# A vision tower: all four score pairs of a half ahead of the feed-forward tiles

## The reference, cut to what matters

```python
for l in range(LAYERS):                       # LAYERS = 6
    keys = jnp.concatenate([past, x], axis=1)
    q = (x @ Wq.T + bq).reshape(B, T, HEADS, HEAD_DIM)        # 16 heads of 16
    k = (keys @ Wk.T + bk).reshape(B, T + H, HEADS, HEAD_DIM)
    v = (keys @ Wv.T + bv).reshape(B, T + H, HEADS, HEAD_DIM)
    scores = jnp.einsum('bqhd,bkhd->bhqk', q, k) / jnp.sqrt(jnp.asarray(HEAD_DIM, x.dtype))
    scores = jnp.where(valid[None, None], scores, neg)
    attn = jax.nn.softmax(scores, axis=-1)
    o = jnp.einsum('bhqk,bkhd->bqhd', attn, v).reshape(B, T, C)
    o = o @ Wo[l].T + bo[l]
    x = _ln(x + o, ln1_g[l], ln1_b[l])
    ff = jax.nn.gelu(x @ W1[l].T + b1[l], approximate=False) @ W2[l].T + b2[l]   # 256 -> 1024 -> 256
    x = _ln(x + ff, ln2_g[l], ln2_b[l])
```

## Time and profile before

| what | us |
|---|---|
| median of 3 runs | 821.38 (821.06 to 822.22) |
| span of the profiled execution | 819.1 |
| TensorE busy in it | 801.5 |
| VectorE busy | 633.9 |
| ScalarE busy | 460.6 |
| GpSimd busy | 251.6 |

### The profile page before, as it was taken

One profiled execution on the slowest core, in us unless ns is written; L12 is line 12 of the kernel. 1 busy time (PEld: TensorE's weight loads), 2 busy tenths in 40 slices (PEclk: granted clock), 3 DMA queues, 4 the chain that ended last, 5 costly groups with the idle time before them and its releaser, 6 DMA issues.

```text
span 819.1 us, 16629 instructions
## 1 busy us (share of the span) xinstructions
PE 801.5 (98%) x6060; PEld 751.4 (92%) x6060; DVE 633.9 (77%) x1287; ACT 460.6 (56%) x829; POOL 251.6 (31%) x297
## 2 busy tenths in 40 slices
PE   9999999999999999999999999999999999999988
PEld 8998789999999999899999989999998999999758
DVE  5786693778778876778797887878778787876796
ACT  4386424433333336585786777667687767745421
POOL 0002120410111100364366147335525623633020
PEclk9999999999999999999999999999999999999999
DMA  5010946998889812010210021031012103010001
GB/s 191 1 52 1 373 124 253 328 323 310 317 309 337 321 53 107 1 40 14 100 44 0 17 98 38 13 102 38 4 39 72 38 13 102 26 82 1 1 0 30
DMA packets 18290, 88.36 MB, mean 108 GB/s; under 512 B 3120, under 2 KB 7472, under 8 KB 12240
## 3 DMA queue, kind: packets, MB, share of 16 engines
q1 hardware_dynamic: 18256, 87.90, 30.4%
HBM read 85.05 MB, written 2.84 MB: 107 GB/s over the span
## 4 chain that ended last, share of the span: by engine, by line
PE 47%; issue 23%; POOL 18%; DVE 8%; ACT 3%; DMA 1%; POOLq 0%; SPq 0%; DVEq 0%; ACTq 0%
PE bank L1139 14%; POOL W_L L2000 7%; PE bank L1176 6%; POOL HF_L L2058 4%; POOL arena L1981 3%; POOL WQKV_L L2000 3%; PE bank L746 2%; PE bank L872 2%; PE bank L1185 2%; PE bank L722 2%; PE bank L1049 2%; PE bank L788 1%; POOL SQ L2019 1%; PE bank L1123 1%; PE bank L1490 1%
## 5 line engine op out<-in xcount | busy, mean ns | idle before, releaser
L1139 PE MATMUL bank<-arena 128*128 (+1 forms) x1024 | 117.8, 274 | 0.0
L1139 PEld LDWEIGHTS bank<-arena 128*128 128x128 f32 x1024 | 117.4, 192 | 0.0
L1981 POOL TENSOR_TENSOR arena<-arena,srec 111x456 f32<-111x456 f32 x56 | 52.3, 962 | 125.1 <-DVE srec L2153 125.1
L2000 POOL TENSOR_TENSOR W_L<-LW,W_H 128x256 fp32r<-128x256 f32 x96 | 68.5, 752 | 36.9 <-DVE XHL L2589 33.5
L2058 POOL TENSOR_TENSOR HF_L<-arena,HF_H 128x296 fp32r<-128x296 f32 x48 | 43.8, 937 | 76.7 <-ACT HF_H L1896 76.7
L788 PE MATMUL bank<-XHL,W_H 128*128 128x296 f32 x288 | 65.1, 307 | 0.0
L1896 ACT ACTIVATE arena<-bank,vec 128x296 f32<-128x296 f32 x96 | 48.8, 509 | 20.4 <-PE bank L788 15.4
L2012 POOL TENSOR_TENSOR QW<-QW,arena x14 | 22.4, 1600 | 119.0 <-DVE QW L2490 65.6
L1330 PE MATMUL bank<-HF_L,W_H 128*128 128x296 f32 x192 | 57.4, 299 | 0.0
L1330 PE MATMUL bank<-HF_H,W_H 128*128 128x296 f32 x192 | 57.4, 299 | 0.0
L1330 PE MATMUL bank<-HF_H,W_L 128*128 128x296 f32 x192 | 57.3, 299 | 0.0
(11 more groups left out here) (276 smaller groups left out, 2205.4 us busy)
## 6 DMA issues: line engine op xcount, KB each, us to landing
arena<-ew_in SPq DMA_DIRECT2D x16, 2048.0 KB, 9.0
arena<-ew_in SPq DMA_DIRECT2D x16, 1024.0 KB, 7.0
LW<-lw_in SPq DMA_DIRECT2D x12, 1024.0 KB, 5.0
arena<-route SPq DMA_DIRECT2D x32, 185.0 KB, 3.2
LW<-lw_in SPq DMA_DIRECT2D x6, 768.0 KB, 4.3
fp_weights<-arena SPq DMA_DIRECT2D x1, 2048.0 KB, 6.4
arena<-fp_weights SPq DMA_DIRECT2D x1, 2048.0 KB, 7.2
arena<-patches_in SPq DMA_DIRECT2D x2, 864.0 KB, 7.4
```

The lines of the kernel that those rows point to most:

```text
L1139: last = mm(o[:, m * CAP:(m + 1) * CAP], w[:, kc, mi * P:(mi + 1) * P], xg(kc, e), start=(kc == 0), stop=(kc == C - 1))
L1981: nc.gpsimd.tensor_tensor(v, v, srec[0:QROWS, s:s + 2, :].unsqueeze(3).to_broadcast([QROWS, 2, C * JH, KEYS]), ALU.mult).then_inc(p_ready, 1)
L2000: last = nc.gpsimd.tensor_tensor(low[:, cols], value[:, cols], high[:, cols], ALU.subtract)
```

## The change

All four pairs of scores stand ahead of the first `f1` tile, both in the list that deals out the banks and in the row that TensorE issues. Before, pairs 0 and 1 stood there, pair 2 behind tiles 0 and 1, and pair 3 behind tiles 2 and 3.

```diff
@@ phase_order
     att("v", 0, 1, 2, 3)
-    att("s", 0, 1)
+    att("s", 0, 1, 2, 3)
     for i in range(4):
         ffn("f1", 2 * i, 2 * i + 1)
-        if i < 2:
-            att("s", 2 + i)
     ffn("f2", 0, 1)
@@ phase, TensorE
                 if x:
-                    for i in range(2):
+                    for i in range(HB // 2):
                         scores(rx, plan, p0 + i)
                 if y:
                     pe.wait_ge(wl_ready["w1"], ly + 1)
...
                     if not x and i == 1:
                         turn_x(0)
-                    if x and i < 2:
-                        scores(rx, plan, p0 + 2 + i)
                 if y:
                     pe.wait_ge(wl_ready["w2"], ly + 1)
                     down()
```

## The result

| | before | after |
|---|---|---|
| median of the runs of one comparison, us | 821.36 (5 runs, 821.06 to 822.22) | 828.11 (5 runs, 827.95 to 828.73) |
| ratio, 95% interval | | 1.0084 (1.0072 to 1.0096) |
| span of the profiled execution, us | 819.1 | 826.9 |
| first score of the first double step to the last product of the last feed-forward, us | 403.08 | 410.07 |
| first score to down projection, half 0 in the feed-forward, us | 10.78 | 11.39 |

The change costs 6.75 us between the medians; 828.2 us was forecast. The spans differ by more, 7.8 us: the first double step's first score starts at 352.90 us before and at 353.74 after, 0.84 us that arise ahead of all that the change touches. In the traces of the eleven experiments, with either order of the scores, this start lies between 353.19 and 353.78 us, so the trace of before was an early one. From there on it is 6.99 us.

What follows compares the result with a forecast made beforehand. TensorE, busy 98% of the span, was taken as the bound, with VectorE's shifts (1.08 us a pair against 0.82 us a tile) making it wait: 6 x 0.60 + 5 x 0.64 = 6.8 us on 821.4 gives 828.2 us, range 823.5 to 830.2 us.

Steps and rivals of the forecast that it cites:

- three waits for shifts: TensorE's tiles 3, 4 and 5 wait for VectorE's shifts 1, 2 and 3: nearly 0, 0.17 and 0.38 us.
- the first wait: Tile 3 could start at 500.70, when shift 1 ends, and starts at 500.76: nearly 0.
- 6 x 0.60 + 5 x 0.64: Down projection starts 0.60 us later in six steps and 0.64 us later in five: 6.8 us in all.
- The restarts: TensorE's starts after waiting for a shift, taken as pair 3's restart shows: 0.06 us behind the shift's end.
- the two bounds: Waiting tile loses nothing at its start, 0.9 us less; or three waits each cost another 0.06 us, 2.0 us more.
- The 2.3 us that the prediction puts around the span: Median of 821.4 us less the profiled span of 819.1 us, said to be untouched by the change.
- the wait of 0.34 us: TensorE's wait for GpSimd's normalise before the last transpose (513.32): said to stay and hide nothing, products and chain moving alike.
- ScalarE's pace: Rival: sixteen gelus start 1.98 us later and end 0.08 or 0.33 us later; 2.1 us, 823.5 us; chance 0.08.
- TensorE's row alone: Rival: evacuations always over in time, step costs 10.50 us on TensorE; 1.8 us less, 819.6 us; chance 0.05.
- Its condition: For the rival on TensorE's row: shift 3 ends before tile 5's own turn, 502.34, and gelus take under 0.39 us.
- Low halves beside GpSimd's pieces of the weights: Rival: meeting on SBUF doubles VectorE's two low halves, 0.75 us in six steps; 4.5 us, 832.7 us; chance 0.03.
- The clock: Rival: short waits halve TensorE's clock for the tiles, 5.2 us a step, 57 us, 885 us in all; chance 0.02.

Runs made afterwards that it cites:

- experiment 1: Kernel after, with VectorE's shift 3 put ahead of the low halves of tiles 0 and 1: 825.40 us, ratio 1.0048.
- experiment 2: Kernel after, with VectorE doing each shift as early as its maximum allows, then all four low halves: 824.78 us, ratio 1.0043.
- experiment 7: Kernel after, with VectorE making the low halves of tiles 0 and 1 twice in the eleven double steps: 836.71 us, ratio 1.0185.
- experiment 8: Kernel before, with VectorE making the low halves of tiles 0 and 1 twice in the eleven double steps: 821.47 us, ratio 1.0001.
- experiment 10: Kernel after, with each reciprocal on VectorE following its own row sum: 824.18 us, ratio 1.0038.
- experiment 5: Kernel of experiment 2, with ScalarE leaving out the f32 gelu of tiles 0 and 1 in the double steps: 821.62 us, ratio 1.0003.
- experiment 4: Kernel before, with pair 2's scores alone moved ahead of the first tile, pair 3 left behind tiles 2 and 3: 838.27 us, ratio 1.0205.

## Why the prediction was right

*The cause.* Forecast were three waits for shifts in each of eleven steps, because VectorE shifts a pair in 1.08 us and TensorE does a tile in 0.82 us. The kernel after's rows show them, and experiments 1, 2 and 7 test them: moving VectorE's instructions takes TensorE's loss away in full, and doubling the two low halves adds their length to the time in full. Only the first wait, put at nearly 0, is missing in six of the steps, where tile 3 finds shift 1 done.

*The places.* Counted from the step's first score, tiles 4 and 5 were put at 7.54 and 8.83 us and measured at 7.54 and 8.83; down at 11.38 and 11.17 us, measured 11.39 and 11.17. The waits were put at nearly 0, 0.17 and 0.38 us from the products' starts; the row of weight loads calls them 0.18, 0.23 and 0.46 us. The low halves of tiles 0 and 1 took their 0.375 us each, as taken.

*The sum.* 6 x 0.60 + 5 x 0.64 = 6.8 us against 6.75 us between the medians and 6.99 us between the traces. The restarts cost what pair 3's had shown, 0.06 us behind a shift: the measured time lies between the two bounds, 827.3 and 830.2 us. The 2.3 us that the prediction puts around the span are too much: the traced execution of after has a span of 826.9 us and took 828.73 us, 1.8 us more, so the trace of before belongs to an execution some 0.5 us faster than the median. The forecast is a difference added to the median, so this doesn't enter it.

*The chain behind.* That the gelus and the last transpose move by what down moves, so that the wait of 0.34 us hides nothing, held in the rows (0.61 and 0.62 us). Experiments 8 and 10 show why it matters: a delay of the products alone is hidden by that wait, and the changed kernel has both late alike.

*The rivals.* ScalarE's pace was no bound of the changed kernel, but it is the next one: experiment 2 brought it up, with the gelus late by 0.07 and 0.31 us where 0.08 and 0.33 were worked out. Its price of 2.1 us was too small, 3.4 us measured, because it left out that GpSimd's fourth normalise then falls behind RSUM, some 0.22 us in each of six steps. TensorE's row alone (819.6 us) was not reached: with the row of experiment 2 and ScalarE relieved it was 821.6 us. Its condition alone was not enough. In the steps of experiment 5 with half 1 in the feed-forward shift 3 ends 7.93 us behind the first score and tile 5 starts at 8.00 us, its own turn, and yet down starts at 10.54 us, since that tile takes 0.91 us instead of 0.82. Whether another row of VectorE does better stays open. Low halves beside GpSimd's pieces of the weights did not meet: the pieces ended 0.6 us ahead. The clock stayed at 1.00 in all three stretches, and in experiment 4 with a pause of 1.26 us a step. The rows that the prediction points to have no pause above 0.34 us; the trace of before has one of 0.81 us, at 341.06, with the clock at 1.00 from 339 to 343.

*What the prediction did not say.* That the new wait shows on the page as 0.2 us a step only, a third of the loss.

## What to carry to other kernels

When jobs rotate through a few banks, look at which engine empties each bank and in which order it does so: a block of jobs with the same emptier goes at that engine's pace where that is the slower one, and what stands between two evacuations on its list (here two low halves) is paid by the engine that fills. A delay is hidden by a later wait only if it moves one of the two sides that meet there. Ahead of a wait on a chain, look for two results that are made in a batch where the first could be passed on at once: here that was worth 0.41 us a step, 0.5% of the kernel.

## What the runs showed of the hardware

- Of a late start only a part is called idle on TensorE's matmul row: tile 5 waited 0.46 us by the row of the weight loads and 0.22 us by that of the matmuls. Total waits for shifts by the matmul row were 2.3 us, by the row of weight loads 8.3 us (1.3 us before), where the traces differ by 6.99 us.
- Which of two engines pays for a meeting on SBUF depends on who began: RSUM on VectorE took 1.11 us behind GpSimd's normalise and 0.51 us ahead of it, and then the normalises took 0.22 us longer. In experiment 1, where the two began within 0.02 us of each other, both outcomes occurred in one execution, 0.30 us apart.
- Sixteen transposes in a row go up to the next product in 1.70 us; with a wait of 0.34 us ahead of the last four it was 2.11 us, so the restart itself cost 0.07 us. A tile whose weights could not be loaded ahead costs 0.085 us more than one whose were (0.905 against 0.82 us in the kernel before; 0.91 to 0.93 us in experiment 5).
